# Second layer's maximum scans over two half super-blocks at once, the second half backwards

## The reference

```python
e = alpha_src[row] + alpha_dst[col]
m = jax.ops.segment_max(e, col, num_segments=n)
e_exp = jnp.exp(e - m[col])
s = jax.ops.segment_sum(e_exp, col, num_segments=n)
att = e_exp / (s[col] + 1e-16)
out = jax.ops.segment_sum(att[:, :, None] * x_proj[row], col, num_segments=n)
```

## Time and profile before

| | us |
|---|---|
| runs shown, median (lowest to highest) | 3578.93 (3575.56 to 3579.14) |
| the profiled execution's own time | 3576.32 |
| its span in the trace | 3574.6 |
| first gather of layer 0 starts | 95.8 |
| second layer's first and last gather start | 2085.6 and 3114.7 |

### The profile page before, as it was taken

How to read it: one execution, slowest core, us unless ns; L and a number is a source line. 1 busy time by engine, 2 the same in 40 slices (tenths; PEclk the granted TensorE clock), 3 DMA queues, 4 the chain that set the end, 5 groups by cost and what they waited for, 6 DMA issues and landing times. The chain is left out here.

```text
span 3574.6 us, 54480 instructions
## 1 busy us (share of the span) xinstructions
PE 2776.7 (78%) x13194; PEld 2280.1 (64%) x13195; DVE 1849.9 (52%) x4502; ACT 1146.4 (32%) x4187; POOL 1719.6 (48%) x1811
## 2 busy tenths in 40 slices
PE   1477788888876699999999437777677776768999
PEld 0366666666664588888888325555555554557888
DVE  4324454454557211111111747888888888866664
ACT  3001010000001122222222235555555556534554
POOL 0777777777771123222222057777777777600000
PEclk9988888898887899999999768888888888888999
DMA  5333334333331222222221634433333334300000
GB/s 163 114 105 111 109 109 116 110 110 109 110 110 32 77 83 86 87 83 86 88 85 34 191 106 110 108 105 108 105 106 104 107 106 110 92 21 14 19 19 21
DMA packets 152340, 327.85 MB, mean 92 GB/s; under 512 B 38839, under 2 KB 90001, under 8 KB 148034
## 3 DMA queue, kind: packets, MB, share of 16 engines
q0 software_dynamic: 85824, 236.38, 23.5%
q1 hardware_dynamic: 53494, 76.64, 6.3%
q10 hardware_dynamic: 12844, 12.82, 1.1%
HBM read 286.42 MB, written 41.40 MB: 92 GB/s over the span
## 5 line engine op out<-in xcount | busy, mean ns | idle before, releaser
L684 POOL DMA_INDIRECT G<-g_rows,srcT x784 | 742.7, 947 | 392.6 <-issue 236.7
L684 POOL DMA_INDIRECT G<-h_rows,srcT x784 | 753.3, 961 | 238.8 <-issue 237.6
L849 PE MATMUL pS<-G,O 128*128 x2336 | 565.1, 406 | 169.4 <-issue 98.2
L1760 PE MATMUL pS<-G,O 128*128 x2336 | 627.2, 431 | 37.8 <-DVE O L1908 29.8
L849 PEld LDWEIGHTS pS<-G,O 128*128 128x128 f32 x2336 | 473.7, 205 | 257.3 <-issue 180.0
L1760 PEld LDWEIGHTS pS<-G,O 128*128 128x128 f32 x2336 | 485.0, 211 | 174.6 <-issue 62.9
L1825 ACT ACTIVATE G<-G 128x32 f32<-128x32 f32 x2352 | 503.2, 307 | 0.0
L1418 ACT ACTIVATE HE<-pH,b1s 128x256 f32<-128x256 f32 x432 | 204.4, 473 | 584.2 <-PE pH L1393 584.2
L1393 PE MATMUL pH<-XT,w1s 128*128 128x256 f32 x1728 | 384.2, 381 | 1.2 <-SPq L1364 1.2
L1403 PE MATMUL pY<-w2s,HE 128*128 128x256 f32 x1728 | 382.0, 380 | 0.0
L1325 POOL DMA_INDIRECT y_rows<-YE,yidx x108 | 109.3, 1012 | 527.8 <-DVE YE L1445 511.4
(11 more groups left out here) (292 smaller groups left out, 3512.4 us busy)
## 6 DMA issues: line engine op xcount, KB each, us to landing
w1s<-in_W_dram SPq DMA_DIRECT2D x16, 1024.0 KB, 4.9
w2s<-in_W_dram SPq DMA_DIRECT2D x16, 1024.0 KB, 7.8
G<-h_rows,srcT POOLq DMA_INDIRECT x784, 2.8
Y<-y_rows SPq DMA_DIRECT2D x49, 256.0 KB, 4.6
G<-g_rows,srcT POOLq DMA_INDIRECT x784, 2.8
g_rows<-OUT SPq DMA_DIRECT2D x49, 132.0 KB, 2.4
h_rows<-ACC SPq DMA_DIRECT2D x7, 896.0 KB, 4.0
out_dram<-X SPq DMA_DIRECT2D x48, 128.0 KB
```

The source lines that it names most:

```text
L684: pool.indirect_dma_start(out=G[:, c % (ring * Q), 0:width], out_offset=None, in_=rows, in_offset=bass.IndirectOffsetOnAxis(ap=srcT[:, c:c ...
L849: mm = nc.tensor.matmul(pS[k][:, 0:W], O[:, k, q, :], G[:, bass.ds((s % R0) * Q + q, 1), :].rearrange("p a d -> p (a d)"), start=(q == 0), ...
L1760: mm = nc.tensor.matmul(pS[:, bass.ds((w % BANKS) * BANK, NR)], O[:, k, q, :], G[:, bass.ds((s % R) * Q + q, 1), 0:NR].rearrange("p a d -> ...
```

## The change

The last 4 chunks of each super-block are stored backwards in the turned lists, in the order of the chunks and within each chunk (`rows_b` with `back`, beside `rows_f` with `front`), for all that reads `srcT`, `dstT` and `lastT`. The scores of the first half go to the first 16 partitions and those of the second to partitions 32 to 47, so that one scan of 512 elements on 48 partitions runs forwards in the first half and backwards in the second. Two copies then hand each side the other's last value (`partner`), with which the second scan starts. `FL` is loaded by six transfers a batch. The rest follows the new layout. Core of the diff:

```diff
+    gaps_back = scratch("gaps_back", (z.RG * P * P,), F32)
...
-            gaps = sb("gaps", [P, z.RG, P])
+            gaps = sb("gaps", [P, 2, z.RG, P])
+            front = sb("front", [P, P])
+            back = sb("back", [P, P])
+            rows_b = sb("rows_b", [P, 3, z.RG, P])
...
                 loc.link(nc.vector.tensor_scalar(rows_f[:, 2, :, P - 1:P], rows_f[:, 2, :, P - 1:P], q_last[:, 0:1],
                                                  None, ALU.max))
 
-                loc.link(nc.vector.tensor_scalar(gaps[:], rows_f[:, 2], -FAR, None, ALU.mult))
+                by_super = lambda m: m[:].rearrange("p (s q) -> p s q", q=Q)
+                loc.tick(nc.vector.memset(front[:], 0.0))
+                loc.link(nc.vector.memset(back[:], 0.0))
+                loc.tick(nc.vector.tensor_copy(by_super(front)[:, :, 0:Q // 2], by_super(ident)[:, :, 0:Q // 2]))
+                loc.link(nc.vector.tensor_copy(by_super(back)[:, :, Q // 2:Q], by_super(ident)[:, :, Q // 2:Q][:, :, ::-1]))
+                loc.link(nc.vector.tensor_copy(rows_b[:], rows_f[:, :, :, ::-1]))
                 loc.eng.sem_inc(s_rowsf, 1)
+                loc.tick(nc.vector.tensor_scalar(gaps[:, 0], rows_f[:, 2], -FAR, None, ALU.mult))
+                loc.link(nc.vector.tensor_scalar(gaps[:, 1], rows_f[:, 2, :, ::-1], -FAR, None, ALU.mult))
+                loc.eng.sem_inc(s_rowsf, 1)
 
             def store_gaps(sp, s_rowsf, s_gaps):
-                sp.wait_ge(s_rowsf, 1)
-                sp.dma_start(seg_gaps.rearrange("(g p e) -> p g e", p=P, e=P), gaps[:]).then_inc(s_gaps, 16)
-                sp.wait_ge(s_gaps, 16)
+                sp.wait_ge(s_rowsf, 2)
+                for n, to in enumerate((seg_gaps, gaps_back)):
+                    sp.dma_start(to.rearrange("(g p e) -> p g e", p=P, e=P), gaps[:, n]).then_inc(s_gaps, 16)
+                sp.wait_ge(s_gaps, 32)
...
@@ -270,7 +283,9 @@
                     n, g = divmod(t, z.RG)
                     if t >= 2:
                         pe.wait_ge(s_copied, t - 1)
-                    nc.tensor.transpose(pT[t % 2][:, 0:P], rows_f[:, n, g, :], ident[:]).then_inc(s_turned, 1)
+                    nc.tensor.matmul(pT[t % 2][:, 0:P], rows_f[:, n, g, :], front[:], start=True, stop=False)
+                    nc.tensor.matmul(pT[t % 2][:, 0:P], rows_b[:, n, g, :], back[:], start=False, stop=True)\
+                        .then_inc(s_turned, 1)
...
-            CHUNKS = -(-z.E // P)
+            CHUNKS = NS * Q
...
+            HALF, HQ = z.SE // 2, Q // 2
+            SIDES = 32 + BR
...
-                FL = sb("FL", [BR, z.SE + 1])
-                M2 = sb("M2", [BR, z.SE])
-                SCO = sb("SCO", [P, 2, Q, z.BS, HEADS])
+                FL = sb("FL", [SIDES, HALF + 1])
+                M2 = sb("M2", [64, HALF])
+                partner = sb("partner", [SIDES, 1])
+                SCO = sb("SCO", [P, 2, HQ, 2, 32])
...
-                pA = ps("pA9", [P, Q * P])
+                pA = ps("pA9", [P, HALF])
                 pM = ps("pM9", [P, 512])
-                EXP0 = Q * BR
+                EXP0, EXPN = Q * 32, Q * BR
...
                     def _(sp):
 
                         def load(b):
-                            v = seg_gaps[bass.ds(b * (BC * P), BC * P)].rearrange("(s e) -> s e", s=z.BS)
-                            sp.dma_start(FL[:, 1:z.SE + 1], v.unsqueeze(1).to_broadcast([z.BS, HEADS, z.SE]))\
+                            ahead = seg_gaps[bass.ds(b * (BC * P), BC * P)].rearrange("(s e) -> s e", s=z.BS)
+                            sp.dma_start(FL[0:BR, 1:HALF + 1],
+                                         ahead[:, 0:HALF].unsqueeze(1).to_broadcast([z.BS, HEADS, HALF])).then_inc(s_dr, 16)
+                            back = gaps_back[bass.ds(b * (BC * P), BC * P)].rearrange("(s e) -> s e", s=z.BS)
+                            for j in range(HQ):
+                                q = Q - 1 - j
+                                sp.dma_start(FL[32:SIDES, j * P:(j + 1) * P],
+                                             back[:, q * P:(q + 1) * P].unsqueeze(1).to_broadcast([z.BS, HEADS, P]))\
+                                    .then_inc(s_dr, 16)
+                            sp.dma_start(FL[32:SIDES, HALF:HALF + 1],
+                                         ahead[:, HALF - 1:HALF].unsqueeze(1).to_broadcast([z.BS, HEADS, 1]))\
                                 .then_inc(s_dr, 16)
+                        sp.wait_ge(s_padded, 1)
                         load(0)
                         with sp.Fori(1, z.NB) as b:
                             sp.wait_ge(s_max, b + 0)
...
                         def turn_scores(b, k):
-                            pe.wait_ge(s_sco, b + 1)
-                            for q in range(Q):
-                                tr = nc.tensor.transpose(pA[0:BR, q * P:(q + 1) * P],
-                                                         SCO[:, k % 2, q].rearrange("p s h -> p (s h)"), ident[:])
+                            pe.wait_ge(s_sco, 2 * b + 2)
+                            for j in range(HQ):
+                                tr = nc.tensor.transpose(pA[0:64, j * P:(j + 1) * P],
+                                                         SCO[:, k % 2, j].rearrange("p f r -> p (f r)"), ident[:])
                             tr.then_inc(s_at, 1)
...
-                            for q in range(Q):
-                                tr = nc.tensor.transpose(pM[:, q * BR:(q + 1) * BR], M2[:, q * P:(q + 1) * P],
-                                                         ident[0:BR, 0:BR])
+                            for j in range(HQ):
+                                tr = nc.tensor.transpose(
+                                    pM[:, 0:EXP0].rearrange("p (f j r) -> p f j r", f=2, r=32)[:, :, j],
+                                    M2[:, j * P:(j + 1) * P], ident[0:64, 0:64])
                             tr.then_inc(s_mt, 1)
...
                         def scores(k, i):
                             for s in range(z.BS):
                                 act.wait_ge(s_gath[k * z.BS + s], i * (16 * Q) + 16 * Q)
-                            nc.scalar.activation(SCO[:, k % 2], gates(k), ACT.Copy).then_inc(s_sco, 1)
+                            for f in range(2):
+                                nc.scalar.activation(
+                                    SCO[:, k % 2, :, f, 0:BR].rearrange("p j (s h) -> p j s h", s=z.BS),
+                                    gates(k)[:, f * HQ:(f + 1) * HQ], ACT.Copy).then_inc(s_sco, 1)
...
-                            nc.scalar.activation(pM[:, EXP0:2 * EXP0].rearrange("p (s q h) -> p q s h", q=Q, h=HEADS),
+                            nc.scalar.activation(pM[:, EXP0:EXP0 + EXPN].rearrange("p (s q h) -> p q s h", q=Q, h=HEADS),
...
+                        act.wait_ge(s_padded, 1)
                         batches(act, lambda: scores(0, 0), batch, lambda b: items(span(act, b)))
 
                     @block.vector
                     def _(dve):
                         loc = Local(dve, s_dve)
+                        loc.tick(nc.vector.memset(SCO[:], 0.0))
+                        loc.tick(nc.vector.memset(M2[:], 0.0))
+                        loc.tick(nc.vector.memset(partner[:], 0.0))
+                        loc.link(nc.vector.memset(FL[:], 0.0))
+                        loc.link(nc.vector.memset(FL[0:BR, 0:1], -FAR))
+                        dve.sem_inc(s_padded, 1)
                         loc.tick(nc.vector.memset(ACC[:], 0.0))
                         loc.tick(nc.vector.memset(MR[:], -BIG))
-                        loc.tick(nc.vector.tensor_copy(iota_p, iota_n[:]))
-                        loc.link(nc.vector.memset(FL[:, 0:1], -FAR))
+                        loc.link(nc.vector.tensor_copy(iota_p, iota_n[:]))
...
                         def scans(b, meanwhile=lambda: None):
 
-                            dve.wait_ge(s_dr, b * 16 + 16)
+                            dve.wait_ge(s_dr, (b + 1) * (16 * (HQ + 2)))
                             dve.wait_ge(s_at, b + 1)
-                            loc.tick(nc.vector.tensor_tensor_scan(pA[0:BR, :], FL[:, 0:z.SE], pA[0:BR, :], -BIG, ALU.add, ALU.max))
+                            loc.tick(nc.vector.tensor_tensor_scan(pA[0:SIDES, :], FL[:, 0:HALF], pA[0:SIDES, :], -BIG,
+                                                                  ALU.add, ALU.max))
                             got = meanwhile()
                             loc.settle()
-                            loc.link(nc.vector.tensor_tensor_scan(M2[:, ::-1], FL[:, 1:z.SE + 1][:, ::-1], pA[0:BR, ::-1], -BIG,
-                                                                  ALU.add, ALU.max))
+                            loc.tick(nc.vector.tensor_copy(partner[0:BR], pA[32:SIDES, HALF - 1:HALF]))
+                            loc.link(nc.vector.tensor_copy(partner[32:SIDES], pA[0:BR, HALF - 1:HALF]))
+                            loc.link(nc.vector.tensor_tensor_scan(M2[0:SIDES, ::-1], FL[:, 1:HALF + 1][:, ::-1],
```

(11 more changed lines are left out.)

## The result

| | before | after |
|---|---|---|
| median of 7 runs each (lowest to highest), us | 3579.14 (3575.56 to 3587.74) | 3564.16 (3562.31 to 3569.34) |
| profiled execution, own time and span | 3576.32, 3574.6 | 3562.46, 3560.7 |
| first gather of layer 0 starts | 95.8 | 103.6 |
| second layer's first and last gather start | 2085.6, 3114.7 | 2094.0, 3097.5 |
| PE's first turn of the last stage | 3185.0 | 3165.0 |

The ratio is 0.9954, 95% interval 0.9943 to 0.9965: faster by 0.46% (15 us), where 41 us were forecast. 3564 lies above the range.

The account below looks back on a forecast made before the run. DVE's serial chain was taken as the bound, with POOL's gathers 2.5 us behind per two batches. Gathers -45, tail -2 and set-up +7.5 gave -39.5 from 3576.3, 3536.8, plus one for the runs: 3538 us, range 3522 to 3560.

Parts of the forecast that it names:

- The bound and its move: Second layer: DVE's chain bounds at 42.5 us per two batches, falls to 38.8, under POOL's 40.0, so gathers bound.
- The set-up: Before the first layer: reversed lists, second gaps operation and double turns add 7.5 us (4 to 13).
- Tail: After the second layer's last gather: the last batch's own scans get shorter, -2 us.
- FL's loads: SP's six transfers a batch for one: 7.1 us to land, hidden under 12.2 us of cover, no cost.
- the rival that they come late: FL's six transfers land one after another, 18.6 us against 12.2 of cover; 3650 us, chance 0.06.
- The gathers: Second layer's gathers on POOL: 50 us of waits come back except 5, so -45 us.
- The change shortens this leg: From ACT's scores to every second batch's ninth gather: four fewer PE transposes save 0.94 us, perhaps only 0.47.
- The wait becomes 0 to 0.4 us, I take 0.1 over 23 such spots: POOL's remaining wait for PE at the ninth gather of every second batch, from 0.7 us before.
- -50 + 5: Second layer's gathers: 50 us of POOL's waits removed, 5 us left, 3 of them in batches 43 to 46.
- the earlier start may give only half back: PE at 1.2 GHz after idling: removing four transposes may gain 0.47 us rather than 0.94 before the ninth gather.
- the prediction's own rule: Ninth gather: without a wait it starts 8.45 us after the batch lands; a leg from the scores beyond that is wait.
- ring stays tight: Rival: the 0.7 us wait at the ninth gather of every second batch stays; 3552 us, chance 0.15.

Follow-up runs that it names:

- the memset runs: Changed kernel plus unneeded DVE memsets between the two scans of each batch: one of 640 elements, 3557.8 us; two of 960, 3612.86 us.
- the 29 dummies: Changed kernel plus 29 unused PE matmuls behind M2's transposes, in even batches only: 3548.86 us, ratio 0.9908.
- 18 dummies: Changed kernel plus 18 unused PE matmuls behind M2's transposes, in every batch: 3560.47 us, ratio 0.9942.

## Why the prediction was wrong

**The bound and its move: right.** DVE's chain at 42.5 us per two batches was the bound (the memset runs show the crossing), scans came at 1.22 and 1.27 us for the forecast 1.21, the copies at 0.15, and ACT's scores wait for the gathers in every other batch. More partitions cost nothing that shows, 48 for 16. The Trainium skill (DVE: opcode table, instruction layouts, handler registers and perf-mode slots, section 6), cited there for a cost that goes with the length, is borne out: 2.28 us for 1024 elements, 1.22 for 512.

**The set-up: right.** +7.8 us for the +7.5 of the forecast. DVE's part of it, in the timeline of the set-up after:

```profile
32.13 0.17 DVE L264 MEMSET front<- 128x128 f32 x1
...
32.80 2.95 DVE L268 COPY rows_b<-rows_f 128x2688 f32<-128x2688 f32 x1
35.90 0.63 DVE L270 TENSOR_SCALAR gaps<-rows_f 128x896 f32<-128x896 f32 x1
36.44 1.08 DVE L271 TENSOR_SCALAR gaps<-rows_f 128x896 f32<-128x896 f32 x1
```

The four small operations took 0.67 us (forecast 0.7), `rows_b` 2.95 (2.97, by the rate of L255 and not that of L251); the rest, 4 us by subtraction, is the second gaps operation and the double turns together, which were put at 0.5 + 3.5.

**Tail: right** (-2.8 for -2). **FL's loads: right.** SP's timeline for one batch:

```profile
2591.80 0.65 SPq L1760 DMA_DIRECT2D FL<-seg_gaps  x1
2592.64 3.10 SPq L1765 DMA_DIRECT2D FL<-gaps_back  x4
2595.92 0.62 SPq L1768 DMA_DIRECT2D FL<-seg_gaps  x1
```

The last of the six is issued 4.1 us after the first, and no wait of DVE in the stage is for them. The Trainium skill (DMA: Bandwidth & Descriptors, Bandwidth) spoke against six small transfers; whatever they cost their queue (no row shows when they land), here it is hidden, and the rival that they come late, 0.06, is refuted.

**The gathers: wrong.** The step that failed is "The change shortens this leg: four transposes of SCO for eight, 1.88 us for 8, minus 0.94", or half of it, and from it "The wait becomes 0 to 0.4 us, I take 0.1 over 23 such spots" and -50 + 5. Measured is 0.87 us a spot, 23.8 in all with 4.6 in batch 46, where the alternation breaks (forecast 3; it was 4.7 before), and -25.5 in the gathers' span for -45. The leg was priced from two spots at 9.2 and 9.1 us, the longest and the third longest of a leg that ran from 7.6 to 9.2 with a mean of 8.37, less transposes that stood on no path: PE's first item starts 1.7 us behind the first transpose with four or with eight. And the same removal lengthened the item itself by 0.84 us (5.36 to 6.20), since PE's clock is at the lower level for 6.25 us from the first transpose on, where it was 4.6. The text had both facts in hand, that PE starts there at 1.2 GHz and that "the earlier start may give only half back"; it took the clock as a discount on a gain, when it was a loss with no gain beside it. As a sum: with the leg at 9.26 the prediction's own rule, 9.26 - 8.45 = 0.81 us at 22 of the 23 spots and 4.6 at the one in batch 46, gives 0.81 x 22 + 4.6 = 22 us of waits, and 979 + 22 = 1001 us for the gathers' span, where 1003.5 were measured.

The rival **"ring stays tight"** is what happened, in mechanism and nearly in size: 0.7 us a spot, 3552 us, chance 0.15. It named PE's first item on the slow clock as one cause, though not that the fewer transposes make it slower. It deserved far more: the trace before had the wait of 0.68 us with no lateness at all, and what spoke against it was only that half of the transposes go.

**What remains** between forecast and result for the profiled execution, 3562.5 - 3536.8 = 25.7 us: 19.5 in the gathers, 6.1 in the last stage's two values, +0.9 ahead of the second layer's first gather (8.4 for 7.5), -0.8 in the tail. Of the 6 us nothing was forecast, and the range's width had nothing for them either. What differs in that stage is PE's granted clock, in the windows from its first turn to the end, before and then after:

```profile
3185.00:3574.60 389.60, 361.82 (x2548) 0.96 0.05 18
```

```profile
3165.00:3560.70 395.70, 367.05 (x2548) 0.94 0.05 17
```

The same 2548 records of matmuls are busy 5.2 us longer, and all ten profiles have 0.96 with the short value and 0.94 with the long one. Their clocks part early: in the four short ones the clock first comes to 1.00 9.3 to 9.7 us after the first turn, in the six long ones 9.9 to 10.4 us after it, and these then spend 44 us of the stage at 1.2 GHz and not 31. At half the speed 13 us cost 6.5, about what the two values differ by. What shifts the first rise stays open, and I made no run on it. Each profile is one execution of another kernel, so they don't show either whether one kernel takes both values.

## What to carry to other kernels

Once the bound moves, a leg that was covered before decides, so measure it over all its instances and not at one or two; and take a removed instruction off a leg only if what comes next starts earlier without it. Work on PE just ahead of the critical matmuls isn't only a cost: after an idle time it decides at which clock they run, so fewer instructions there can be slower, as here by some 0.8 us of the first item at a tight spot. Where a ring's slot is given back by one instruction, putting that one first on its engine can pay (18 us here), but not where the engine that it needs is itself the bound (48 us lost).

## What was not expected of the hardware

- Doubling four transposes, 0.85 us more of PE work on the path, made the kernel 13 us faster, and 29 matmuls that nothing reads made it 14 us faster. In each case the granted clock at the first item is what differs: 0.50 for 5.3 to 6.5 us from the time PE resumed with the changed kernel's four transposes (mean 6.25), for 2.8 to 6.2 us with eight (mean 4.8), and 1.00 throughout when PE had no idle time before. The Trainium skill (TensorE: Matmul & The Clock Gate, Part 1) says that the throttled state is the default and activity releases it; the rows agree. That it is the 0.6 us gap between the four transposes and the item that puts the rise off by 1.4 us on average is my guess; no run has the gap alone.
- Some 1.7 us pass between PE's first transpose and the first item's matmul even when only 1.06 us of matmuls lie between; with the 29 dummies in front, PE's queue being fed meanwhile, 0.64 us do. The clock isn't the reason, since it is 1.7 us too at the five spots with 18 dummies where the clock stayed at 1.00. With eight transposes, 1.91 us of matmuls, the 1.7 us stay and nothing is lost. That the time is PE's sequencer working through the item's waits is my reading; no run shows it by itself.
- A copy of f32 with a reversed axis, 128x2688, took 2.95 us, 1.1 ns an element, against 1.56 for the forward cast from int32 of the same size (no run has the same copy forwards); a tensor_scalar over 896 elements took 0.63 us forwards and 1.08 with its input reversed.
